# One semaphore increment per step from TensorE in the edge gather of a graph and expert layer

## The reference

```python
h = xn @ W_layer.T + b_layer
a1, a2 = h @ w_a1.T + b_a1, h @ w_a2.T + b_a2
v = leaky_relu(a1[src] + a2[dst])
att = softmax of v over the edges with the same src     # row = src, col = dst
x = x + segment_sum(att * h[dst], src) + mix(xn)
x = x + experts(layernorm(x))
```

## Time and profile before

| | us |
|---|---|
| median of three runs | 2687.87 |
| the three runs | 2682.23, 2687.87, 2695.58 |
| profiled execution | 2691.85 |
| its span, first to last instruction | 2690.1 |
| its mean granted TensorE clock | 0.871 |

### The profile page before, as it was taken

How to read it: one execution, slowest core, us unless ns; L and a number is a source line. 1 busy time by engine, 2 the same in 40 slices (tenths; PEclk the granted TensorE clock), 3 DMA queues, 4 the chain that set the end, 5 groups by cost and what they waited for, 6 DMA issues and landing times.

```text
span 2690.1 us, 46160 instructions
## 1 busy us (share of the span) xinstructions
PE 2279.7 (85%) x12642; PEld 1883.7 (70%) x12659; DVE 1771.5 (66%) x5731; ACT 1263.3 (47%) x3795; POOL 1283.9 (48%) x1320
## 2 busy tenths in 40 slices
PE   3789848888888788788777787778999999999997
PEld 2566626666666566566655565667999999999997
DVE  8677747777777777777776776777555555455553
ACT  7666645555555555555555555551222222222221
POOL 0000045666666666666665666106444444444443
PEclk7899968877787987888887878758999999999999
DMA  2344333443444344444443434491222222222221
GB/s 79 90 137 121 119 87 96 112 110 105 110 113 112 107 109 113 110 107 109 110 113 98 113 106 86 96 321 37 35 34 37 34 34 37 35 35 36 36 34 26
DMA packets 141988, 237.92 MB, mean 88 GB/s; under 512 B 29547, under 2 KB 101067, under 8 KB 140971
## 3 DMA queue, kind: packets, MB, share of 16 engines
q0 software_dynamic: 65664, 143.64, 23.8%
q1 hardware_dynamic: 76074, 91.34, 10.9%
HBM read 182.34 MB, written 52.53 MB: 87 GB/s over the span
## 4 chain that ended last, share of the span: by engine, by line
PE 54%; issue 15%; DVE 15%; another core or an unknown queue 6%; DVEq 4%; ACT 3%; DMA 2%; POOL 0%; SPq 0%; ACTq 0%; POOLq 0%
PE psum L1705 19%; PE psum L1198 10%; PE psum L1738 10%; DVE arena L1297 3%; PE psum L524 3%; DVEq L1316 3%; PE psum L1189 3%; PE psum L1206 2%; PE psum L503 1%; DVE arena L1308 1%; DVE arena L1341 1%; DVE arena L1603 1%; ACT arena L595 1%; DVE arena L1280 1%
## 5 line engine op out<-in xcount | busy, mean ns | idle before, releaser
L1149 POOL DMA_INDIRECT arena<-table,arena x878 | 848.5, 966 | 505.9 <-issue 235.3
L1198 PE MATMUL psum<-arena 128*128 128x257 f32 x1756 | 665.0, 501 | 233.4 <-issue 108.9
L1198 PEld LDWEIGHTS psum<-arena 128*128 128x128 f32 x1756 | 354.9, 235 | 444.0 <-issue 349.6
L1297 DVE SCALAR_TENSOR_TENSOR arena<-arena,psum 128x257 f32 x878 | 421.4, 480 | 251.2 <-remote 155.0
L1705 PE MATMUL psum<-arena 128*128 128x128 f32 x4620 | 552.0, 276 | 0.6 <-ACT arena L1760 0.6
L1705 PEld LDWEIGHTS psum<-arena 128*128 128x128 f32 x4620 | 542.7, 193 | 6.7 <-issue 0.9
L1835 POOL DMA_INDIRECT out<-arena x105 | 170.6, 1625 | 382.4 <-ACT arena L1767 379.5
L1225 ACT ACTIVATE arena<-arena 128x128 f32<-128x128 bf16 x880 | 280.9, 390 | 117.9 <-DVE arena L1311 86.8
L1738 PE MATMUL psum<-arena 128*128 x1260 | 290.7, 379 | 0.8 <-ACT arena L1767 0.8
L1189 PEld LDWEIGHTS psum<-arena 128*128 128x128 f32 x1760 | 264.4, 223 | 29.8 <-issue 24.0
L1238 ACT ACTIVATE arena<-arena 128x128 f32<-128x128 bf16 x880 | 281.2, 391 | 7.1
(11 more groups left out here) (344 smaller groups left out, 3131.1 us busy)
## 6 DMA issues: line engine op xcount, KB each, us to landing
mix_inputs<-arena SPq DMA_DIRECT2D x147, 128.0 KB, 2.2
arena<-table,arena POOLq DMA_INDIRECT x878
arena<-in_x SPq DMA_DIRECT2D x98, 128.0 KB, 2.9
arena<-mix_inputs SPq DMA_DIRECT2D x49, 256.0 KB
arena<-in_w SPq DMA_DIRECT2D x6, 1364.0 KB, 6.6
out<-arena SPq DMA_DIRECT2D x50, 128.0 KB, 3.3
table<-arena SPq DMA_DIRECT2D x49, 129.0 KB, 2.2
arena<-mix_inputs SPq DMA_DIRECT2D x49, 128.0 KB, 3.1
```

The source lines that it names most:

```text
L1149: pool.indirect_dma_start(rows_in[j][:, q * TW:(q + 1) * TW], None, table_d[:, :], bass.IndirectOffsetOnAxis(ap=col_all[:, t:t + 1], axis=0))\
L1198: mm(psum[4 + q][:, 0:C + 1], weight[b][:, q * P:(q + 1) * P], rows_in[g][:, q * TW:q * TW + C + 1], start=True, stop=True).then_inc(S("pr ...
L1297: v.scalar_tensor_tensor(here, here, alpha[(j - 5) % RING][:, q:q + 1], psum[4 + q][:, 0:C + 1], ALU.mult, ALU.add).then_inc(S("acc_done"), 1)
```

## The change

TensorE raises one semaphore, `pe_step`, once per step, with the last instruction of the step. `mix_done`, `value_done`, `edge_done`, `product_done` and `masked_turned` are gone from the gather. The other engines wait for a number of steps of TensorE instead: VectorE once per step, ahead of its first add and behind `hot` and the register load, for all of TensorE's step i - 1; GpSimd for TensorE's step i - 4; ScalarE for step i - 2 ahead of `masked` and for step i - 1 ahead of the weights and of `member`. No matmul, transfer or operation of another kind is added, removed or moved.

```diff
--- before.py
+++ after.py
@@ -1142,8 +1142,8 @@
                     if i == RING - 3:
                         pool.wait_ge(S("kw_done"), 1)
 
-                    if due((i - RING + 1) * G):
-                        pool.wait_ge(S("product_done"), (i - RING + 1) * G)
+                    if due(i - RING + 1):
+                        pool.wait_ge(S("pe_step"), i - RING + 5)
                     for q in range(REST if i == NG - 1 else G):
                         t = i * G + q
                         pool.indirect_dma_start(rows_in[j][:, q * TW:(q + 1) * TW], None, table_d[:, :],
@@ -1163,7 +1163,6 @@
                     for c in range(2):
                         last = mm(psum[2][:, C:2 * C], mix_q[m % MS][:, c * P:(c + 1) * P], kw_sb[:, c * C:(c + 1) * C],
                                   start=(c == 0), stop=(c == 1))
-                    last.then_inc(S("mix_done"), 1)
                 m = mix_at(i - 1)
                 if m is not None:
                     pe.wait_ge(S("z_ready"), i - 3)
@@ -1171,7 +1170,6 @@
                     for c in range(2):
                         last = mm(psum[3][:, C:2 * C], mix_n[m % MS][:, c * P:(c + 1) * P], wvo_sb[:, c * C:(c + 1) * C],
                                   start=False, stop=(c == 1))
-                    last.then_inc(S("value_done"), 1)
                 if live(i, 2):
 
                     b, t = j % 2, i - 2
@@ -1188,15 +1186,14 @@
                     for q in range(G):
                         last = mm(psum[2 + b][:, 2 * q:2 * q + 2], member[b][:, q * P:(q + 1) * P], lb[b][:, q:q + G + 2:G + 1],
                                   start=True, stop=True)
-                    last.then_inc(S("edge_done"), 1)
                 if live(i, 4):
                     b, g, t = j % 2, (j - 4) % RING, i - 4
                     for q in range(REST if t == NG - 1 else G):
                         pe.wait_ge(S("weight_ready"), t * G + q + 1)
                         if due((t - 1) * G + q + 1):
                             pe.wait_ge(S("acc_done"), (t - 1) * G + q + 1)
-                        mm(psum[4 + q][:, 0:C + 1], weight[b][:, q * P:(q + 1) * P], rows_in[g][:, q * TW:q * TW + C + 1],
-                           start=True, stop=True).then_inc(S("product_done"), 1)
+                        last = mm(psum[4 + q][:, 0:C + 1], weight[b][:, q * P:(q + 1) * P], rows_in[g][:, q * TW:q * TW + C + 1],
+                                  start=True, stop=True)
                 if live(i, 0):
                     b = j % 2
                     if due(i - 1):
@@ -1204,7 +1201,7 @@
                     for q in range(G):
                         pe.wait_ge(S("masked_ready"), i * G + q + 1)
                         last = nc.tensor.transpose(psum[b][:, q * P:(q + 1) * P], masked[b][:, q * P:(q + 1) * P], ident[:, :])
-                    last.then_inc(S("masked_turned"), 1)
+                last.then_inc(S("pe_step"), 1)
 
             steady(pe, step, 4)
 
@@ -1220,7 +1217,7 @@
 
                     act.wait_ge(S("hot_ready"), i + 1)
                     if due(i - 1):
-                        act.wait_ge(S("masked_turned"), i - 1)
+                        act.wait_ge(S("pe_step"), i - 1)
                     for q in range(G):
                         a(masked[j % 2][:, q * P:(q + 1) * P], hot[j][:, q * P:(q + 1) * P], ACT.Copy,
                           scale=a2s[j % 2][:, q:q + 1]).then_inc(S("masked_ready"), 1)
@@ -1232,8 +1229,8 @@
                         act.wait_ge(S("weight_ready"), (t - 1) * G)
                     a(wexp[b][:, :], zarg[:, :], ACT.Exp).then_inc(S("wexp_ready"), 1)
                     act.wait_ge(S("wexp_ready"), t + 1)
-                    if due((t - 1) * G):
-                        act.wait_ge(S("product_done"), (t - 1) * G)
+                    if due(t - 1):
+                        act.wait_ge(S("pe_step"), t + 3)
                     for q in range(G):
                         a(weight[b][:, q * P:(q + 1) * P], hot[(j - 3) % RING][:, q * P:(q + 1) * P], ACT.Copy,
                           scale=wexp[b][:, q:q + 1]).then_inc(S("weight_ready"), 1)
@@ -1241,8 +1238,7 @@
                     b = (j - 1) % 2
                     act.wait_ge(S("max_done"), i)
                     if due(i - 2):
-                        act.wait_ge(S("edge_done"), i - 2)
-
+                        act.wait_ge(S("pe_step"), i)
                     a(member[b][:, :], psum[b][:, :], ACT.Sign).then_inc(S("member_ready"), 1)
                     act.wait_ge(S("dm_ready"), i)
                     if due((i - RING) * G):
@@ -1268,7 +1264,6 @@
                 pm = psum[2 + b][:, 0:2 * G].rearrange("p (q c) -> p q c", c=2)
                 if part == 0:
                     gv = rows_in[(j - 3) % RING].rearrange("p (q c) -> p q c", c=TW)
-                    dve.wait_ge(S("edge_done"), t + 1)
                     if due(t):
                         dve.wait_ge(S("wexp_ready"), t)
                     v.tensor_tensor(score[:, :], pm[:, :, 0], gv[:, :, C + 1], ALU.add).then_inc(S("z_steps"), 1)
@@ -1290,7 +1285,6 @@
                     dve.wait_ge(S("acc_cleared"), 1)
                 if q == 0:
                     dve.wait_ge(S("alpha_ready"), t + 1)
-                dve.wait_ge(S("product_done"), t * G + q + 1)
                 if due(t * G + q):
                     dve.wait_ge(S("acc_done"), t * G + q)
                 here = acc[:, bass.ds(columns[q], C + 1)]
@@ -1316,18 +1310,16 @@
                     _, columns = nc.values_load_multi_w_load_instructions(
                         bt_i[0:1, ds((i - 5) * G, G)], engines=(dve.engine,), min_val=0, max_val=(NT - 1) * TW,
                         skip_runtime_bounds_check_because="the table holds first columns of buckets")
+                if due(i):
+                    dve.wait_ge(S("pe_step"), i)
                 add(i, j, 0, columns)
                 exponents(i, j, 0)
                 if live(i, 1):
                     b, t = (j - 1) % 2, i - 1
-                    if due(t - 1):
-                        dve.wait_ge(S("edge_done"), t - 1)
                     v.tensor_copy(lb[b][:, 0:G], a1t[:, ds(t * G, G)])
                 add(i, j, 1, columns)
                 exponents(i, j, 1)
                 if live(i, 1):
-
-                    dve.wait_ge(S("masked_turned"), t + 1)
                     if due(t):
                         dve.wait_ge(S("nb_steps"), t)
                     v.tensor_reduce(tile_max[:, :], psum[b].rearrange("p (q r) -> p q r", q=G)[:, :, :], AX.X, ALU.max)\
@@ -1350,14 +1342,12 @@
                                            ALU.subtract, ALU.add).then_inc(S("lin_steps"), 1)
                 m = mix_at(i - 1)
                 if m is not None:
-                    dve.wait_ge(S("mix_done"), m + 1)
                     dve.wait_ge(S(f"mix_in{m % MS}"), m // MS * 32 + 32)
                     v.scalar_tensor_tensor(mix_b[m % MS], psum[2][:, C:2 * C], fac[:, m:m + 1], mix_b[m % MS], ALU.mult, ALU.add)\
                         .then_inc(S("part_ready"), 1)
                 m = mix_at(i - 2)
                 if m is not None:
                     dve.wait_ge(S("part_ready"), m + 1)
-                    dve.wait_ge(S("value_done"), m + 1)
                     v.tensor_tensor(mix_b[m % MS], psum[3][:, C:2 * C], mix_b[m % MS], ALU.add).then_inc(S("half_ready"), 1)
                 add(i, j, 3, columns)
                 if live(i, 1):
```

## The result

The changed kernel took 2674.03 us (median of 9 runs, 2672.56 to 2676.64) against 2693.13 us before it on the same chip (9 runs, 2682.23 to 2701.32): a ratio of 0.9934, with a 95% interval of 0.9919 to 0.9949. It is faster by some 19 us, and the forecast was slower by 1.2%. The profiled execution took 2673.89 us for a span of 2672.2.

The account below looks back on a forecast made before the run. The prediction took the gather to be paced by GpSimd's beat, held up by TensorE's late increments. It summed 2691.85 + 0 + 0 + 31 = 2723, less 4 for the median of the runs: 2719 us, slower by 1.2%, range 2560 to 2800.

Parts of the forecast that it names:

- the lateness to go: Rival: in the gather the single increment is no longer late, 5.5 us a step, 123 us faster, 2569 us; chance 0.33.
- The likeliest case: "The beat holds": eight gathers and a pause remain, increment as late as before, 31 us slower, 2688 to 2773; chance 0.45.
- The bound and its cause: Gather stage: GpSimd's beat, eight gathers and a pause, waits for TensorE's late increments; 256.5 us lost in 115 waits.
- The coarse wait, +31 us: Gather: waiting for TensorE's whole step delays GpSimd 0.56 us in one step of four, 31 us; bounds 0 and 85.
- The increments, 0: TensorE in the gather: 6.5 increments a step become one; taken as 0, at most -256.5 us if all pauses go.
- VectorE's waits, 0: VectorE in the gather: six queue instructions of 21 ns a step go, 28 us, hidden by GpSimd's beat, so 0.
- ScalarE's waits and the other stages, 0: ScalarE idles 2.67 us of a gather step, so 0; times outside the gather stay within a microsecond or two.
- The pause after every four gathers: Rival: GpSimd also stops before the beat's fifth gather, 6.95 us a step, slower, 2786 or 2884 us; chance 0.17.
- 2569 and 2435: Times of the rival that the lateness goes: 5.5 us a gather step gives 2569, all pauses gone 2435; chance 0.33.
- 2786 and 2884: Times of the pause-after-four rival: increment late in every second unpaused step, 98 us, or in all, 196 us; chance 0.17.

Follow-up runs that it names:

- two_incs: Changed kernel with two increments a step, one behind the products for GpSimd and VectorE's first add, one at the end: 2673.66 us, ratio 0.9936.
- incs_back: Changed kernel with TensorE's old increments raised again, 5.5 more a step, that nobody waits for: 2678.99 us, ratio 0.9957.
- waits_back: Changed kernel with VectorE's old waits back in their places, seven a step, already met on the new semaphore: 2686.08 us, ratio 0.9979.
- The drain: Changed kernel with the increment raised by a TensorE drain in place of the last transpose: 2479.14, 2487.68 and 2483.54 us on chips B, C and D.
- the half gathers: Changed kernel with gathers of 64 rows in place of 128 from step 16 on: 2440.84, 2450.42 and 2442.65 us on chips B, C and D.
- the plain transfers: Changed kernel with SP's plain transfers of fixed rows in place of GpSimd's gathers: 2428.2, 2440.58 and 2436.06 us on chips B, C and D.
- drain_c: Changed kernel with the step's increment raised by a TensorE drain, run on chip D: 2483.54 us, ratio 1.0098 to the kernel before.

## Why the prediction was wrong

The forecast was slower, and on this chip the change is faster by 0.7%. The range, 2560 to 2800, holds 2674.03 by luck: its lower end was set for the lateness to go, and it stayed. The likeliest case's own range, 2688 to 2773, does not hold it. Step by step:

**The bound and its cause** were read rightly. GpSimd's beat of eight gathers and a pause paces the stage, the waits are "remote" before and after, and TensorE's work was over some 2 us before they ended. That the number of increments is not what makes them late held as well: 18.88 us at the start of the stage against 18.93. What was missed is that VectorE's increments come late too, by up to 2 us.

**The coarse wait, +31 us**, is the step that failed, and the largest miss: it gave the forecast its sign, and two_incs has it at 0. The mechanism was seen: the fifth gather starts at 1004.76, 0.27 us after the transposes that end at 1004.49, within the 0.6 named. But the step added this lateness to the beat. The pause behind the eighth gather is shorter by as much, and two_incs, which takes the lateness away, runs the same time (2673.66 to 2674.03). The lateness was over-sized as well: counted as above, the fifth gathers were late by 17.9 us in the kernel before and are by 32.2 in the changed one, 14 us more and not 31. The text had this as its lower bound, "if the pause absorbs it", and took the four measured steps instead. That chose between absorbed and not absorbed by the size of the delay, which says nothing on it. What speaks on it is what ends the pause, and the prediction had no row for that. What does end it, no run here shows.

**The increments, 0**, was off in size: incs_back has them at 5.0 us of gain. The bounds were 0 and -256.5, and the right value is close to the 0.

**VectorE's waits, 0**, is the other step that failed: waits_back has them at 12.1 us. The cover named for them was that VectorE stands idle in every second step. It does, but the steps between are not idle: there TensorE's products wait for VectorE's additions and for weights that wait for its exponents, and GpSimd's fifth gather for the end of TensorE's step. The text counted 28 us for these instructions, and held that they would come only if the beat broke. The beat did not break and 12 came. With 0 for the coarse wait and these two prices the sum would be 2691.85 - 4 - 17 = 2671 us, against 2674 measured. A cover that exists in one step of two can hide at most what falls into that step, half of the 28 here.

**ScalarE's waits and the other stages, 0**, fit: 17.1 of the 17.9 us are between the first and the last gather. No run takes ScalarE's waits by themselves.

**The rivals.** The pause after every four gathers did not come: of the 106 stretches between two starts over 2 us apart, 104 have eight gathers. In waits_back 53 of 132 have four, so the place that this rival named, the fifth gather, is where delay does gather. The lateness did not go either: 218.0 us of waits of 256.5 remain, and the time is 2674, not 2569. The result lies between the forecast and that case, by small terms that had been set to nothing. (That case's 2569 and 2435 lack the 4 us that the forecast and the 2786 and 2884 take off.)

**How the gain arises in the beat** is argued from the traces, not shown by an experiment. Between the last gather before a pause and the first behind it were 3.07 and 3.33 us; in the changed kernel it is 1011.35 - 1008.51 = 2.84. One explanation is that in the kernel before several increments are due when the lateness ends and GpSimd's is not the first of them. incs_back speaks against it: with the increments raised again the pauses are 1.89 us each against 1.85, where 2.23 were before. Fewer waits of VectorE, and the exchange with the fifth gather, fit the rows better; the rest is open.

**Why increments are late** on two chips and not on three is not settled. The drain, the half gathers and the plain transfers were built to tell, and none of them ran on a chip where they are late. One caution belongs here: the profile models the ends of matmuls, so such an end alone doesn't prove that the work was over. Three things speak for a late increment: at the start of the gather TensorE had run on into the next step's products and transposes, up to 386.56 us, with the increment outstanding until 400.07; VectorE's increments are late as well; and on chips B, C and D none is.

## What to carry to other kernels

A time that the profile puts between the end of a matmul and the instruction that waits for it, and calls "remote", may belong to the chip: run the kernel before on a second one before a change is built against it, and time the change on both. Where two engines take turns in setting the pace, a cover for small costs holds only for the steps in which the covering engine is late; in the other steps instructions that vanish can be worth up to their own length (an estimated 14 us here, half of 28, where 12 were measured). A delay inside a beat costs something only if it moves what ends the beat, so look for that first; and when an idle time shrinks, look whether another grew, before it is called a gain.

## What was not expected of the hardware

The same kernel takes 2693.8, 2664.8, 2458.6, 2459.9 and 2459.7 us on five chips, the medians of 7 to 23 runs each. The runs of one chip lie close together, 2682.23 to 2702.09 on the widest of them, but for a single one of 6594.45 on chip C. On chips A and E TensorE's semaphore increments reach the engines that wait for them 2 to 3 us late while a stream of gathers runs, and up to 19 us late at the start of one, and VectorE's up to 2 us late (102 of 1601 recorded ones by more than 0.5 us in the kernel before, 128 of 1736 in the changed one); in the trace of chip C none is by more than 0.02 us. TensorE itself keeps working meanwhile, up to its next wait.

VectorE's waits whose semaphore has long been raised are not free: 8 ns each in waits_back on average, when some of them lie on a path between engines. The Trainium skill, "VectorE: DVE Perf Modes", section "The DRAIN you can't avoid", has a row of copies take the same time with a semaphore after each as with one at the end. No run here has such a row of copies, so none tests that; the 12.1 us are for waits between engines, where VectorE hands over to TensorE.

A drain on TensorE lasts 502 ns at least and 985 ns in the median where it ends a step of gather work (drain_c), and with one in each step the kernel is 0.9% to 1.4% slower than the kernel before.
